# Group norm of a one-core hybrid block: statistics from a second, transposed load of the input

## The reference

```python
x = x + conv_attention(_gn(x), g, w_qkv, w_out, b_out)       # layer 0, 4 heads of 32
t = tokens(x)
t = t + attention(layernorm(t), W_qkv, b_qkv, W_out, b_out)  # layer 1, causal, 4 heads of 16
t = t + moe(layernorm(t), Wg, bg, W1, b1, W2, b2)            # 8 experts, top 2, exact gelu

def _gn(v, G=32, eps=1e-05):            # 2 neighbouring channels x 256 pixels per group
    m, s = mean and variance over (2, 16, 16) of each image and group
    return (g - m) / jnp.sqrt(s + eps)
# and inside conv_attention, before the product with w_qkv:
xn = x * rsqrt(mean(x * x, axis=1) + 1e-12) * g[None, :, None, None]
```

## Time and profile before

| what | value |
|---|---|
| device time, median of 3 runs | 117.54 us (116.78 to 117.62) |
| the profiled execution's own time | 116.64 us |
| its span, first to last instruction | 114.9 us |
| PE, DVE, ACT, POOL busy | 88%, 64%, 56%, 18% of the span |
| granted TensorE clock, mean | 0.993 |

### The profile page before, as it was taken

One profiled execution on the slowest core, in us unless ns is written; L12 is line 12 of the kernel. 1 busy time (PEld: TensorE's weight loads), 2 busy tenths in 40 slices (PEclk: granted clock), 3 DMA queues, 4 the chain that ended last, 5 costly groups with the idle time before them and its releaser, 6 DMA issues.

```text
span 114.9 us, 2256 instructions
## 1 busy us (share of the span) xinstructions
PE 101.5 (88%) x833; PEld 53.0 (46%) x833; DVE 73.9 (64%) x214; ACT 64.3 (56%) x121; POOL 20.1 (18%) x35
## 2 busy tenths in 40 slices
PE   5955987889999999988889999899999999999920
PEld 2333565645555454656656655466332323232300
DVE  5287379969910846999968578998819552255250
ACT  0414974280588956565156977894957545754400
POOL 6910482000000000000000000000002941443140
PEclk9999999999999999999999999999999999999997
DMA  1810000995000000000000000000000000000003
GB/s 14 254 22 2 0 5 17 245 207 93 0 6 0 0 6 3 0 0 0 6 0 0 6 0 0 0 0 3 0 6 0 0 0 0 0 0 0 6 0 91
DMA packets 6075, 2.85 MB, mean 25 GB/s; under 512 B 4001, under 2 KB 6065, under 8 KB 6065
## 3 DMA queue, kind: packets, MB, share of 16 engines
q1 hardware_dynamic: 5104, 2.19, 9.8%
q10 hardware_dynamic: 960, 0.52, 1.5%
HBM read 2.45 MB, written 0.26 MB: 24 GB/s over the span
## 4 chain that ended last, share of the span: by engine, by line
PE 67%; DVE 15%; ACT 7%; DMA 4%; issue 3%; DVEq 0%
PE bank L914 13%; PE bank L925 13%; PE bank L857 6%; PE bank L790 5%; PE bank L822 5%; DMA x<-in_x_dram 4%; PE bank L871 4%; PE bank L841 3%; PE bank L741 3%; PE bank L732 3%; PE bank L708 2%; DVE mx L577 2%; DVE mx L573 2%; ACT sq L393 2%; PE bank L828 1%
## 5 line engine op out<-in xcount | busy, mean ns | idle before, releaser
L472 ACT ACTIVATE hid<-bank,b1c 128x1024 f32<-128x1024 f32 x16 | 16.9, 1112 | 11.8 <-PE bank L914 11.8
L430 ACT ACTIVATE pr<-bank 128x1024 f32<-128x1024 f32 (+1 forms) x16 | 14.0, 914 | 8.5 <-PE bank L828 5.1
L914 PE MATMUL bank<-xn,w_sb 64*128 64x512 f32 x64 | 15.6, 612 | 0.0
L925 PE MATMUL bank<-hid,w_sb 128*64 128x512 f32 x64 | 15.3, 603 | 0.0
L692 DVE SCALAR_TENSOR_TENSOR yw<-bank,b2c,wc 128x512 f32<-128x512 f32 x8 | 6.0, 748 | 12.6 <-PE bank L925 12.6
L362 POOL TENSOR_TENSOR acc<-yw,x 64x512 f32<-64x512 f32 x1 | 1.3, 1269 | 70.2 <-DVE yw L692 70.2
L708 PE MATMUL bank<-still 128*128 128x512 bf16 (+1 forms) x43 | 10.9, 397 | 2.3 <-DVE still L486 1.3
L573 DVE TENSOR_REDUCE mx<-bank 128x4 f32<-128x1024 f32 x8 | 9.3, 1219 | 1.1 <-PE bank L790 1.0
L367 POOL TENSOR_TENSOR acc<-acc,yw 128x512 f32<-128x512 f32 x6 | 7.6, 1273 | 11.8 <-DVE yw L692 11.6
L914 PEld LDWEIGHTS bank<-xn,w_sb 64*128 64x128 f32 x64 | 5.6, 186 | 8.5 <-ACT hid L472 4.4
L790 PE MATMUL bank<-k,q 32*128 32x256 f32 (+1 forms) x128 | 8.3, 373 | 1.3 <-ACT q L418 0.6
(11 more groups left out here) (148 smaller groups left out, 175.5 us busy)
## 6 DMA issues: line engine op xcount, KB each, us to landing
w_sb<-in_L_ffn_W_dram SPq DMA_DIRECT2D x3, 512.0 KB, 7.8
x<-in_x_dram ACTq DMA_DIRECT2D x1, 256.0 KB, 4.0
x<-in_x_dram SPq DMA_DIRECT2D x1, 256.0 KB, 4.3
bqkv<-in_L_attn_b_qkv_dram SPq DMA_DIRECT2D x12, 0.1 KB, 1.5
wo1t<-in_L_attn_W_out_dram SPq DMA_DIRECT2D x8, 4.0 KB, 1.5
out_dram<-acc SPq DMA_DIRECT2D x1, 128.0 KB, 2.5
out_dram<-acc ACTq DMA_DIRECT2D x1, 128.0 KB, 2.9
wq<-in_L_conv_w_qkv_dram ACTq DMA_DIRECT2D x1, 96.0 KB, 4.1
```

The source lines that it names most:

```text
L430: nc.scalar.activation(pr[:, b, 2 * p:2 * p + 2, 0:n], two(key, 0, n), ACT.Exp, scale=SCALE[l]).then_inc(free(key), 1)
L472: nc.scalar.activation(hid[:, k % 4, :, :], two(("h", 0, k)), ACT.Gelu, bias=b1c[:, k:k + 1]).then_inc(free(("h", 0, k)), 1)
L914: i = mm(ps(key, i=s), w1_sb[r, e, P * j:P * j + P], XN[r, 2 * s:2 * s + 2, :].rearrange("p b t -> p (b t)"), start=True, stop=True)
L925: i = mm(ps(key, p0=C * s, p1=C * s + C), w2_sb[:, k, :], hid[:, k % 4, s, :], start=(j == 0), stop=(j == FT - 1))
```

## The change

It does five things. (1) SP first loads x once more, as `xg`: one row per image and group (4 x 32 = 128 rows) of 512 elements. One `bn_stats` and one `bn_aggr` then give each group's mean and variance directly. `pairs` and its three POOL operations go; DVE builds `place` and `sel` from the identity instead. The inverse root is taken on 128 x 1 tiles before the product, and the product with `sel` now spreads finished scale and shift to the 128 channel rows. (2) Both copies of X are issued on ACT, behind the load of its function table. (3) g is no longer multiplied in on DVE: w_qkv is loaded twice straight into `wg0`, g into a column `gcol`, and ACT's copy of the transposed weights has `gcol` as its scale. These four transfers stand on SP behind `xg`. (4) In layer 0 ACT squares x itself, with scale and bias `gs`; `dev` is still written on DVE (with a factor of -0.5), but only `xr` reads it. (5) `xr` of layer 0 moves from POOL to DVE, the copies of weights on ACT and the last three transposes on PE move to later places, and POOL sets V1 to ones early.

```diff
@@ -117,7 +117,8 @@
             holder[i] = key
     take(("prep_g", 0), 0)
-    take(("prep_t", 0), 2, 2)
+    take(("prep_w", 0), 6)
+    take(("prep_t", 0), 7)
     for step, l, b, banks in ORDER:
...
         def _(sp):
-            sp.dma_start(X[0:C, :, :], xo).then_inc(ld["x"], 16)
+            sp.dma_start(xg[:, :], x.rearrange("b (g r) h w -> (b g) (r h w)", r=2)).then_inc(ld["xg"], 16)
+            for r in range(2):
+                sp.dma_start(wg0[:, :, r, :], wqkv0.rearrange("(t p) c -> p t c", p=P)).then_inc(ld["a"], 16)
+            for p0 in (0, C):
+                sp.dma_start(gcol[p0:p0 + C, :], g0.rearrange("(c o) -> c o", o=1)).then_inc(ld["a"], 16)
             sp.dma_start(wo0[0:C, :], wout0).then_inc(ld["g"], 16)
...
-            def xr_(l, b):
-                if l == 0:
-                    pool.wait_ge(S["r0", l], b + 1)
-                    nc.gpsimd.tensor_tensor(xr[:, b, :], dev[:, b, :], sq[:, b, :], ALU.mult).then_inc(S["xr", l], 1)
...
         def _(act):
-            act.dma_start(X[C:P, :, :], xo).then_inc(ld["x"], 16)
-            act.dma_start(wq0[:, :, :], wqkv0.rearrange("(t p) c -> p t c", p=P)).then_inc(ld["a"], 16)
-            act.dma_start(grow[:, :], g0.partition_broadcast(P)).then_inc(ld["a"], 16)
             nc.scalar.preload_act_table_set("natural_log_exp_and_others")
-            act.wait_ge(stats, 4)
-            nc.scalar.activation(gt[:, 3, :], gt[:, 2, :], ACT.Ln).then_inc(gact, 1)
+            for p0 in (0, C):
+                act.dma_start(X[p0:p0 + C, :, :], xo).then_inc(ld["x"], 16)
+            act.wait_ge(stats, 2)
+            act.wait_ge(cst, 1)
+            nc.scalar.activation(root[:, 0:1], mv[:, 1:2], ACT.Ln, bias=eps[:, 3:4]).then_inc(gact, 1)
             act.wait_ge(gact, 1)
-            nc.scalar.activation(gt[:, 3, :], gt[:, 3, :], ACT.Exp, scale=-0.5).then_inc(gact, 1)
-            def prep_transposed():
+            nc.scalar.activation(root[:, 0:1], root[:, 0:1], ACT.Exp, scale=-0.5).then_inc(gact, 1)
...
+            def prep_qkv():
+                key = ("prep_w", 0)
+                filled(act, key)
+                nc.scalar.activation(w0t[:, :, :], ps(key, 0, 3 * P).rearrange("p (t o) -> p t o", t=3),
+                                     ACT.Copy, scale=gcol[:, 0:1]).then_inc(free(key), 1)
...
             def square(l, b):
-                act.wait_ge(S["dev", l], b + 1)
-                centred = ps(("norm", l, b), 0, T) if l else dev[:, b, :]
-                nc.scalar.activation(sq[:, b, :], centred, ACT.Square).then_inc(S["sq", l], 1)
+                if l:
+                    act.wait_ge(S["dev", l], b + 1)
+                    nc.scalar.activation(sq[:, b, :], ps(("norm", l, b), 0, T), ACT.Square).then_inc(S["sq", l], 1)
+                else:
+                    if b == 0:
+                        act.wait_ge(ld["x"], 32)
+                        emptied(act, ("prep_g", 0))
+                    nc.scalar.activation(sq[:, b, :], X[:, b, :], ACT.Square, scale=gs[:, 0, b:b + 1],
+                                         bias=gs[:, 1, b:b + 1]).then_inc(S["sq", l], 1)
...
-                if (step, l, b) == ("square", 0, 0):
-                    prep_transposed()
+                if (step, l, b) == ('r2', 0, 0):
+                    prep_qkv()
+                if (step, l, b) == ('r2', 0, 1):
+                    prep_rest()
...
+            onehot = ident[:, :].rearrange("p (b g) -> p b g", b=B)
+            nc.vector.tensor_reduce(place[:, :], onehot, AX.X, ALU.add)
+            nc.vector.tensor_reduce(share[:, :], onehot.rearrange("p b g -> p g b"), AX.X, ALU.add).then_inc(link, 1)
+            dve.wait_ge(link, 1)
+            nc.vector.tensor_scalar(sel[:, :].rearrange("p (r g k) -> p r g k", r=2, k=2),
+                                    share[:, :].rearrange("p (r g k) -> p r g k", r=1, k=1).to_broadcast([P, 2, C // 2, 2]),
+                                    -0.5, None, ALU.mult).then_inc(link, 1)
+            dve.wait_ge(ld["xg"], 16)
+            nc.vector.bn_stats(st6[:, :], xg[:, :]).then_inc(stats, 1)
+            dve.wait_ge(stats, 1)
+            nc.vector.bn_aggr(mv[:, :], st6[:, :]).then_inc(stats, 1)
+            dve.wait_ge(stats, 2)
+            nc.vector.tensor_scalar(ve[:, 0:1], mv[:, 0:1], -1.0, None, ALU.mult)
+            nc.vector.tensor_scalar(ve[:, 1:2], mv[:, 1:2], GN_EPS, None, ALU.add).then_inc(link, 1)
+            dve.wait_ge(link, 3)
+            dve.wait_ge(gact, 2)
+            nc.vector.tensor_scalar(root[:, 1:2], root[:, 0:1], ve[:, 1:2], root[:, 0:1], ALU.mult, ALU.mult).then_inc(link, 1)
+            dve.wait_ge(link, 4)
+            nc.vector.scalar_tensor_tensor(root[:, 2:3], root[:, 1:2], -3.0, root[:, 0:1], ALU.add, ALU.mult).then_inc(link, 1)
+            dve.wait_ge(link, 5)
+            nc.vector.tensor_scalar(gr[:, 0, :], place[:, :], root[:, 2:3], None, ALU.mult)
+            nc.vector.tensor_scalar(gr[:, 1, :], place[:, :], root[:, 2:3], ve[:, 0:1], ALU.mult, ALU.mult).then_inc(stats, 1)
+            filled(dve, ("prep_g", 0))
+            gps = ps(("prep_g", 0), 0, 2 * B).rearrange("p (s b) -> p s b", s=2)
+            nc.vector.tensor_copy(gs[:, :, :], gps).then_inc(free(("prep_g", 0)), 1)
+            emptied(dve, ("prep_g", 0))
+            nc.vector.tensor_scalar(gh[:, :, :], gs[:, :, :], -0.5, None, ALU.mult).then_inc(link, 1)
+            dve.wait_ge(link, 6)
             dve.wait_ge(ld["x"], 32)
...
             for b in range(B):
-                i = nc.vector.bn_stats(st6[:, b, :], X[:, b, :])
-            i.then_inc(stats, 1)
-            dve.wait_ge(stats, 1)
-            for b in range(B):
-                i = nc.vector.bn_aggr(mv[:, b, :], st6[:, b, :])
-            i.then_inc(stats, 1)
-            dve.wait_ge(ld["a"], 32)
-            for t in range(3):
-                for r in range(2):
-                    i = nc.vector.tensor_tensor(wg0[:, t, r, :], wq0[:, t, :], grow[:, :], ALU.mult)
-            i.then_inc(prep_v, 1)
-            filled(dve, ("prep_g", 0))
-            gmv = ps(("prep_g", 0), 0, 2 * B).rearrange("p (b s) -> p b s", s=2)
-            nc.vector.tensor_tensor(gt[:, 0, :], mv[:, :, 0], gmv[:, :, 0], ALU.subtract).then_inc(stats, 1)
-            dve.wait_ge(stats, 3)
-            nc.vector.tensor_tensor(gt[:, 1, :], gt[:, 0, :], gt[:, 0, :], ALU.mult).then_inc(link, 1)
-            dve.wait_ge(link, 1)
-            nc.vector.scalar_tensor_tensor(gt[:, 2, :], gt[:, 1, :], GN_EPS, gmv[:, :, 1], ALU.add, ALU.add).then_inc(stats, 1)
-            dve.wait_ge(gact, 2)
-            nc.vector.tensor_tensor(gt[:, 4, :], gt[:, 3, :], gt[:, 3, :], ALU.mult).then_inc(link, 1)
-            dve.wait_ge(link, 2)
-            nc.vector.tensor_tensor(gt[:, 5, :], gt[:, 4, :], gt[:, 2, :], ALU.mult).then_inc(link, 1)
-            dve.wait_ge(link, 3)
-            nc.vector.tensor_scalar(gt[:, 4, :], gt[:, 5, :], -0.5, 1.5, ALU.mult, ALU.add).then_inc(link, 1)
-            dve.wait_ge(link, 4)
-            nc.vector.tensor_tensor(gt[:, 0, :], gt[:, 3, :], gt[:, 4, :], ALU.mult).then_inc(link, 1)
-            dve.wait_ge(link, 5)
-            nc.vector.scalar_tensor_tensor(gt[:, 1, :], gmv[:, :, 0], -1.0, gt[:, 0, :], ALU.mult, ALU.mult).then_inc(free(("prep_g", 0)), 1)
-            emptied(dve, ("prep_g", 0))
-            for b in range(B):
-                nc.vector.tensor_scalar(dev[:, b, :], X[:, b, :], gt[:, 0, b:b + 1], gt[:, 1, b:b + 1],
+                nc.vector.tensor_scalar(dev[:, b, :], X[:, b, :], gh[:, 0, b:b + 1], gh[:, 1, b:b + 1],
                                         ALU.mult, ALU.add).then_inc(S["dev", 0], 1)
...
                 dve.wait_ge(S["r0", l], b + 1)
+                if l == 0:
+                    dve.wait_ge(S["dev", 0], b + 1)
+                    nc.vector.tensor_tensor(xr[:, b, :], dev[:, b, :], sq[:, b, :], ALU.mult).then_inc(S["xr", l], 1)
+                    return
...
             for step, l, b, _ in ORDER:
-                if step == "xr" and l:
+                if step == "xr":
                     xr_(l, b)
...
             pe.wait_ge(still_set, 1)
-            idle(("prep_g", 0), 15)
-            pe.wait_ge(consts, 6)
-            pe.wait_ge(stats, 2)
-            mm(ps(("prep_g", 0), 0, 2 * B), pairs[:, :], mv[:, :, :].rearrange("p b s -> p (b s)"), start=True, stop=True).then_inc(full(("prep_g", 0)), 1)
-            key = ("prep_t", 0)
-            pe.wait_ge(prep_v, 1)
+            idle(("prep_g", 0), 13)
+            pe.wait_ge(link, 2)
+            pe.wait_ge(stats, 3)
+            mm(ps(("prep_g", 0), 0, 2 * B), sel[:, :], gr[:, :, :].rearrange("p s b -> p (s b)"), start=True,
+               stop=True).then_inc(full(("prep_g", 0)), 1)
+            key = ("prep_w", 0)
+            pe.wait_ge(ld["a"], 64)
             for t in range(3):
-                nc.tensor.transpose(ps(key, P * t, P * t + P), wg0[:, t, :, :].rearrange("p r c -> p (r c)"), ident[:, :])
-            pe.wait_ge(ld["g"], 16 * 5)
...
```

(11 more changed lines are left out.)

61 lines of the change are left out of this document (27 added, 34 removed).

## The result

| | median of runs, us | lowest to highest | span of the profiled execution | its own time |
|---|---|---|---|---|
| before | 117.35 | 116.78 to 117.62 | 114.9 | 116.64 |
| changed | 114.72 | 114.57 to 114.85 | 112.8 | 114.85 |

Changed over before: 0.9754, 95% interval 0.9713 to 0.9795. The kernel became 2.6 us faster, against the 2.85 of the forecast (114.5). Between the two profiled executions the difference is smaller: 116.64 - 114.85 = 1.8, by the spans 2.1. So the medians moved by 0.5 more than the span that the traces explain, and that has to be accounted for too. (The ratios in this document leave out single runs that took over 1.5% longer than the fastest of their kernel; medians and ranges have them.)

What follows compares the result with a forecast made beforehand. The prediction took the start, x's load and the group chain up to the first maximum, as the bound: 116.64 - 0.7 (load) - 2.3 (group chain) - 0 = 113.6, median 114.5 us; forecast case 113.5 to 115.2, with gaining rivals 112.9 to 116.3.

Steps and rivals of the forecast that it cites:

- What bounds the kernel: Start to first maximum: the core waits on x's load and group chain; a shift there reaches the end in full.
- The load: Landing of xg: between 3.8 and 5.1, taken as 4.4 instead of X's 5.11, saving 0.7 us.
- the fast bound: Earliest landing of xg: 0.81 + 2.3 + 0.66 = 3.8, with 256 KB moved at 387 GB/s.
- The group chain: From xg's landing to first square: steps sum to 2.68, square at 7.1 instead of 10.14, 3.0 us saved with the load.
- From the square to `project`, and to the maximum: After the first square: ln 1.6 behind it, project 4.4, first maximum 7.55; the 0.3 gained at project is given back.
- the setup on DVE: Before the statistic on DVE: two reductions and sel, 0.35 each, about 1 us from 2.7, within idle time.
- Rival 1: PE waits for late weights, gcol landing 5.7 to 7.6: price 0 to 1.0, late case 114.8 to 115.7, chance 0.18.
- Rival 2: First square waits for X, issued behind ACT's table load: landing 6.9 free, 8.2 gives 115.6; chance 0.05.
- Rival 3: Four xr of 0.42 moved to DVE don't overlap: 1.7 lost, time 116.2, chance 0.07.
- Rival 4: TensorE falls to its lower clock after a PE gap above 1.1: costs 3.5 to 6, 118.7 to 121, chance 0.08.
- The sum: Whole kernel: 116.64 - 0.7 - 2.3 - 0 = 113.6 for the profiled execution, 114.5 as median.
- the 0.9 that was added for the median: Whole kernel: the profiled execution before lay 0.9 below the runs' median, 117.54, taking 113.6 to 114.5.

Runs made afterwards that it cites:

- pool_late: Changed kernel with POOL's three large memsets, both mask selects, w_qk and iota held back until dev is written: 114.54 us.
- v1_late: Changed kernel with only POOL's memset of V1 put back behind dev: 114.68 us.
- pool_late_pe: pool_late with the three w_qkv transposes and their load wait moved behind the third var, 11 fillers instead of 13 and 5 instead of 8: 113.79 us.
- xr_pool: Changed kernel with xr of layer 0 moved back from DVE to POOL: 114.87 us.
- dve_copies_2: pool_late_pe with copies wo0t, b1c and b2c on DVE, ACT's wait for them behind r2 of layer 0's last image: 113.57 us.

## Why the prediction was right, and where it was not

**What bounds the kernel.** Right. The chain from the load to the first square was the place, and the shift of the first maximum, 2.10, was the shift of the span, 2.1.

**The load.** Between the bounds, and better than the value taken: 3.94 and not 4.4, and in `pool_late` it was there by 3.50, when the statistic starts (below the lower bound, 3.8). A gain of 1.2 and not 0.7 at this point. The step that was too cautious is the 227 GB/s of a queue alone: from 2.5 to 3.0 the queues moved 367 GB/s, near the 387 of the fast bound.

**The group chain.** 2.68 was forecast from landing to square; 7.97 - 3.94 = 4.03 was measured. Of the 1.35 too much, 5.33 - 3.94 - 0.69 = 0.70 is `sel` standing ahead of the statistic, an estimate of 0.35 that took 1.51, behind a cast that took 1.44. The rest is small steps: from the aggregate at 5.38 to the square they took 2.59 against 2.0 in the working. Ln and Exp took 0.57 with their start against 0.46, the two `root` steps 0.58 against 0.38, the two writes of `gr` 0.45 against 0.25, and the copy out of PSUM with the hand-over to ACT 0.30 against 0.19; the working had taken each step at its bare length in a row, and left out most of the 0.1 that passing a result between engines took. In seven profiles with a short `sel` and the square taken from x, the square came at 6.9 to 7.2, as the 7.1 of the forecast. This was luck too: `xg` was there 0.6 to 0.9 before the 4.4 taken, and the chain behind it took some 3.3 instead of 2.68.

**From the square to `project`, and to the maximum.** Right in size: 1.49, 4.43 and 7.64 against 1.6, 4.4 and 7.55. But this was so because the square was late. In `pool_late` and `v1_late`, with the square in time, `var` followed it by 1.78 and 1.64, not 0.9. This is the second step that failed, next to the setup on DVE: the forecast let PE's filler start together with the square, and it starts behind the transposes, which need `gcol`. In the changed kernel the two coincide (7.93 and 7.97) because `sel` had delayed the square.

**Rival 1** is thus real, though it came masked. Its sign, `var` over 1.0 behind the square with PE waiting for a transfer, is absent in the changed kernel (0.85) and plain in `pool_late` (1.78, PE idle 0.92 for `gcol`). `gcol` landed near 7.4, close to the 7.6 and 7.5 of its working and not the 5.7, so the reading that the trace's rates speak against such a delay failed: from 4 to 6, with X on one queue and the weights on the other, the transfers moved 188 to 219 GB/s, where the kernel before moved 354, 387 and 325 in the half microseconds from 3.0. Whether the 256-byte pieces of the weights cost this, or both halves of X on one queue, no run separates. The price, of 0 to 1.0, is 0.8 at the maximum (15.48 to 14.69) and 0.75 of time. It and the long `sel` cost the kernel once, not twice, since they overlap. With both taken away, the maximum stood at 14.69; the forecast was 7.1 + 7.55 = 14.65, and the span at 111.9 = 114.9 - 3.0.

**Rival 2** was right on the landing, at no cost in the changed kernel. X came at 6.91 to 7.17 where ACT waited for it; 6.9 was computed. But it came so by two errors that cancel. The table load did not hold the queue: the issues ran from 0.77 to 2.19, beside the load at 0.73 to 2.01. So the drain of 1380 ns that the Trainium skill names (ScalarE: Activation LUTs, What ACT_TABLE_LOAD costs) plays no part in these issues. The second half was issued at 1.56 and not at 2.8, and took 5.48 (in `pool_late_pe`) and not the 4.0 to 4.1 of the working, with `xg` and the weights on their way at the same time.

**Rival 3** did not come; see `xr_pool`. **Rival 4** did not come in the changed kernel, whose PE gap ahead of the product was 0.47 and whose clock read 1.00 in every stretch up to the maximum. The gap was that small because the first fillers ended at 6.84 (7.31 - 0.47) and not at 5.6. Its mechanism was shown by the two runs in which the group chain came late. Gaps of 2.29 and 3.33 were followed by 0.50; the 1.31 of `dve_copies_2` was not.

**The sum.** The sum's 3.0 was 1.8 to 2.1 in the profiled executions, 0.9 to 1.2 too much, and the 0.9 that was added for the median did not apply: most of it was span that the kernel before has in a usual run and the changed kernel, whose profiled execution lies 0.13 above its median, has not. The two errors cancelled: 114.72 against 114.5. The mechanism and its place were right, the hit within 0.2 was partly luck.

## What to carry to other kernels

When a chain starts at a load, look at what else the same engine must wait for in program order: here one wait for 64 counts of `ld["a"]` ahead of a filler took 0.75 of what the faster load had brought, and moving it behind the work that was ready gave it back. The profiled execution of a kernel that waits for a transfer can be a lucky one: compare its span with those of the other runs, and don't carry the difference over to a kernel that no longer waits. An experiment that undoes one part can open a gap on PE and be charged for the clock as well; read the granted clock before taking its loss as the worth of that part. Where an added wait stands ahead of a function that needs a new table, see in the trace whether the table load still lies in idle time.

## What the runs showed of the hardware

- Where DVE's cast of 128 x 128 met a row of POOL memsets, either the first memset took 0.18 instead of 0.10 and the cast 0.28, or the cast ended only behind the whole row: 0.54 with four small memsets, 1.44 with a fifth of 0.96. `sel` took 0.23 with no memset beside it and 1.51 beside two of 0.95.
- A DMA issue on ACT's queue runs beside a table load (0.77 beside 0.73 to 2.01), against my rival 2.
- Two transfers of 64 rows of 4 bytes, behind 448 KB on their queue and beside 512 KB on the other, needed 4.4 and 4.9 from issue to landing; two of the same size later on the queue need 2.3.
- A square of 256 elements on ACT with scale and bias as per-partition operands takes 0.59, without them 0.41.
- In the profile of the changed kernel the first fillers start 0.43 apart until 5.86, the pace of the lower clock level, while the granted clock reads 1.00: 512 columns in 0.43 are 1.2 GHz. The later ones of the same shape take 1.90 for eight, 0.24 each. In the kernel before the quicker pace came after 3.79, not 5.86.
